# A group norm and attention kernel: the setup and the first image in another order

## What is computed

```python
h = group_norm(x)                       # 32 groups of 8 channels, per image
q, k, v = h @ Wq + bq, h @ Wk + bk, h @ Wv + bv
scores = einsum('bnc,bmc->bnm', q, k) * 256 ** -0.5
attn = softmax(scores, axis=-1)
out = x + einsum('bnm,bmc->bnc', attn, v) @ Wo + bo
```

## Time and profile before

| what | value |
|---|---|
| median of 3 runs | 1845.19 us (1845.04 to 1846.48) |
| profiled execution | 1844.48 us, of which the span 1842.8 us |
| PE busy | 1815.6 us, 99% of the span |
| DVE busy | 1663.2 us, 90% |
| ACT busy | 984.1 us, 53% |
| mean granted PE clock | 0.994 |

### The profile page before, as it was taken

How to read it: one execution, slowest core, us unless ns; L and a number is a source line. 1 busy time by engine, 2 the same in 40 slices (tenths; PEclk the granted TensorE clock), 3 DMA queues, 4 the chain that set the end, 5 groups by cost and what they waited for, 6 DMA issues and landing times.

```text
span 1842.8 us, 32692 instructions
## 1 busy us (share of the span) xinstructions
PE 1815.6 (99%) x11562; PEld 1654.1 (90%) x11562; DVE 1663.2 (90%) x2921; ACT 984.1 (53%) x1347; POOL 92.1 (5%) x107
## 2 busy tenths in 40 slices
PE   8899999999999999999999999999999999999997
PEld 7799998999998998989999989989989999899896
DVE  5999999999999999999999999999999999999985
ACT  3645545646546556456455465465564554654652
POOL 0000000000000000000000000000000000000000
PEclk9999999999999999999999999999999999999998
DMA  3111222212222212222122222022221122220211
GB/s 114 58 51 29 68 57 68 68 26 54 68 57 68 62 18 68 57 68 68 36 44 68 57 68 67 12 68 62 63 68 43 37 68 57 68 68 17 62 24 24
DMA packets 29296, 101.92 MB, mean 55 GB/s; under 512 B 3681, under 2 KB 4706, under 8 KB 29282
## 3 DMA queue, kind: packets, MB, share of 16 engines
q0 software_dynamic: 9216, 33.56, 11.7%
q1 hardware_dynamic: 20066, 68.17, 11.2%
HBM read 68.16 MB, written 67.11 MB: 73 GB/s over the span
## 4 chain that ended last, share of the span: by engine, by line
PE 98%; DVE 1%; ACT 0%; DMA 0%; issue 0%; SPq 0%; POOLq 0%
PE ps_s L619 48%; PE ps_o L693 13%; PE ps_o L695 13%; PE ps_o L694 13%; PE ps_o L619 10%; DMA s_buf<-in_L_conv_bq_dram 0%; ACT p_hi L312 0%; ACT s_buf L318 0%; DVE s_buf L485 0%; DVE p_lo L493 0%; PE ps_o L631 0%; DVE s_buf L510 0%; DVE query_max L472 0%; SPq L217 0%; POOLq L66 0%
## 5 line engine op out<-in xcount | busy, mean ns | idle before, releaser
L693 PE MATMUL ps_o<-v_hi,p_hi 128*128 128x258 f32 x2048 | 580.6, 283 | 2.8 <-DVE p_lo L493 2.8
L695 PE MATMUL ps_o<-v_hi,p_lo 128*128 128x258 f32 x2048 | 581.1, 284 | 0.0
L694 PE MATMUL ps_o<-v_lo,p_hi 128*128 128x256 f32 x2048 | 578.4, 282 | 0.0
L312 ACT ACTIVATE p_hi<-s_buf 128x1024 fp32r<-128x1024 f32 x256 | 272.0, 1063 | 527.5 <-DVE s_buf L485 527.5
L619 PE MATMUL ps_s<-g_hi,h_hi 128*128 128x512 f32 x1024 | 399.7, 390 | 7.8 <-ACT s_buf L304 7.7
L619 PE MATMUL ps_s<-g_hi,h_lo 128*128 128x512 f32 x1024 | 400.4, 391 | 0.0
L619 PE MATMUL ps_s<-g_lo,h_hi 128*128 128x512 f32 x1024 | 399.8, 390 | 0.0
L693 PEld LDWEIGHTS ps_o<-v_hi,p_hi 128*128 128x128 f32 x2048 | 389.2, 190 | 5.7 <-issue 2.2
L694 PEld LDWEIGHTS ps_o<-v_lo,p_hi 128*128 128x128 f32 x2048 | 388.9, 190 | 3.0
L695 PEld LDWEIGHTS ps_o<-v_hi,p_lo 128*128 128x128 f32 x2048 | 388.7, 190 | 0.0
L304 ACT ACTIVATE s_buf<-ps_s 128x512 f32<-128x512 f32 x512 | 292.9, 606 | 170.2 <-PE ps_s L619 166.3
(11 more groups left out here) (84 smaller groups left out, 2199.5 us busy)
## 6 DMA issues: line engine op xcount, KB each, us to landing
x_t<-in_x_turned_dram SPq DMA_DIRECT2D x64, 512.0 KB, 3.9
out_dram<-in_x_dram SPq DMA_DIRECT2D x64, 512.0 KB, 7.3
out_dram<-o_buf POOLq DMA_DIRECT2D x64, 512.0 KB, 5.6
s_buf<-in_L_conv_Wq_dram SPq DMA_DIRECT2D x1, 256.0 KB, 3.0
s_buf<-in_L_conv_Wk_dram SPq DMA_DIRECT2D x1, 256.0 KB, 3.0
s_buf<-in_L_conv_Wv_dram SPq DMA_DIRECT2D x1, 256.0 KB
s_buf<-in_L_conv_Wo_dram SPq DMA_DIRECT2D x1, 256.0 KB
s_buf<-in_L_conv_bq_dram SPq DMA_DIRECT2D x1, 1.0 KB, 3.1
```

Of the source, the lines that this page charges most:

```text
L312: nc.scalar.activation(p_hi[c][:, rows, :], s_buf[c][:, rows, :], ACT.Exp, scale=SCALE).then_inc(p_hi_done, 1)
L693: nc.tensor.matmul(ps[:, 0:VC], p_hi[c][:, m, cols], v_hi[:, m, :], start=m == 0, stop=False)
L694: nc.tensor.matmul(ps[:, 0:C], p_hi[c][:, m, cols], v_lo[:, m, :], start=False, stop=False)
L695: last = nc.tensor.matmul(ps[:, 0:VC], p_lo[c][:, m, cols], v_hi[:, m, :], start=False, stop=m == T - 1)
```

## The change

SP issues `x_t` of image 0 ahead of the weights, and the three short bias vectors behind them with semaphores of their own. PE multiplies two constant tiles twelve times into an unused bank, then transposes all three weights and does both folds ahead of `project_g`. ACT, no longer DVE, copies the transposed weights out. In image 0, `normalise`, `h_parts` and `h_rest` work by halves of 512 tokens, half 0 first. DVE now does the whole group norm of image 1 between `g_rest` and `part_maxima` of image 0, and the `v_lo` parts after the first `difference`. ACT puts the copies of the first four score tiles of half 1 between the exponentials of half 0. The loop over images 1 to 30 and the last image are untouched.

```diff
+            load_turned(0)
             load_weight(0, wq, wqk_in)
             load_weight(1, wk, wqk_in)
-            with nc.allow_non_contiguous_dma(reason="a short vector, once"):
-                sp.dma_start(bq_col, bq.rearrange("(k p) -> p k", p=P)).then_inc(wqk_in, 16)
-            load_turned(0)
             load_weight(2, wv, wvo_in)
             load_weight(3, wo, wvo_in)
...
+                sp.dma_start(bq_col, bq.rearrange("(k p) -> p k", p=P)).then_inc(bq_in, 16)
+                sp.dma_start(bv_col, bv.rearrange("(k p) -> p k", p=P)).then_inc(bias_in, 16)
+            sp.dma_start(bo_row, bo.rearrange("(a n) -> a n", a=1)).then_inc(bias_in, 16)
...
+            turned_out(0)
+            turned_out(1)
+            turned_out(2)
+            first_h_part(0, 0, first_h, first_h_hi)
+            first_h_part(1, 0, first_h, first_h_hi)
+            fold_first(a_hi, ps_a, 1)
+            first_h_part(0, 1, h_done, h_hi_done)
+            first_h_part(1, 1, h_done, h_hi_done)
+            fold_first(vo_hi, ps_vo, 3)
...
+            def first_softmax():
+
+                for i in range(4):
+                    v_part(0, i)
+                exponentials_hi(0, 0, 0)
+                scores_out(0, 1, 0)
+                exponentials(0, 0, 0)
+                scores_out(0, 1, 1)
+                exponentials_hi(0, 0, 1)
+                scores_out(0, 1, 2)
+                exponentials(0, 0, 1)
+                scores_out(0, 1, 3)
+                for i in (2, 3):
+                    exponentials_hi(0, 0, i)
+                    exponentials(0, 0, i)
+                for m in range(4, T):
+                    scores_out(0, 1, m)
...
+            first_normalise(0, 0, first_h)
+            first_normalise(1, 0, first_h)
+            first_normalise(0, 1, h_done)
+            first_normalise(1, 1, h_done)
+            first_h_rest(0, 0, first_h_hi, first_h_lo)
+            first_h_rest(1, 0, first_h_hi, first_h_lo)
+            fold_rest(0, a_hi, a_lo, ps_a)
+            dve.wait_ge(bias_in, 16 * 2)
...
+                channel_stats(1)
+                dve.wait_ge(bn_done, 8)
+                channel_sums(1)
+                group_means(1)
+                group_spread(1)
+                maxima(0, 0, 0)
+                group_variance(1)
+                maxima(0, 0, 1)
+                turn_back(1)
+                maxima(0, 0, 2)
+                normalise(1)
+                maxima(0, 0, 3)
+                maxima(0, 0, 4)
...
-            pe.wait_ge(wqk_in, 16 * 3)
             pe.wait_ge(const_step, 7)
+            for _ in range(12):
+                nc.tensor.matmul(ps_idle[:, 0:P], ident[:], ones[:], start=True, stop=True)
+            pe.wait_ge(wqk_in, 16 * 2)
             turn_weight(0)
             turn_weight(1)
-
+            pe.wait_ge(wvo_in, 16 * 2)
+            turn_weight(2)
             pe.wait_ge(w_turned, 2)
             fold(ps_a, wq_t, wk_t)
```

More of the change, by code:

```diff
@@ L287, in h_parts, with first_h_part @@
                     nc.scalar.activation(h_hi[:, k, :], x_t[:, k, :], ACT.Copy).then_inc(h_hi_done, 1)
+            def first_h_part(k, c, ready, done):
+                act.wait_ge(ready, k + 1)
+                cols = slice(c * Q, (c + 1) * Q)
+                nc.scalar.activation(h_hi[:, k, cols], x_t[:, k, cols], ACT.Copy).then_inc(done, 1)
             def g_part(b, i):
@@ L354, in body @@
                 if first:
[L355 to L361, removed]
+                    first_softmax()
+                else:
+                    softmax_beside(b, 0, lambda i: v_part(b, i))
+                    scores_out(b, 1, 0)
+                    last_exponentials(b, 0)
+                    for m in range(1, T):
+                        scores_out(b, 1, m)
                 if not last:
@@ L424, in normalise, with first_normalise, first_h_rest @@
                                             ALU.subtract, ALU.mult).then_inc(h_done, 1)
+            def first_normalise(k, c, done):
+                cols = slice(c * Q, (c + 1) * Q)
+                nc.vector.tensor_scalar(x_t[:, k, cols], x_t[:, k, cols], norm[:, 0, k:k + 1], norm[:, 1, k:k + 1],
+                                        ALU.subtract, ALU.mult).then_inc(done, 1)
+            def first_h_rest(k, c, ready, done):
+                cols = slice(c * Q, (c + 1) * Q)
+                dve.wait_ge(ready, k + 1)
+                nc.vector.tensor_tensor(h_lo[:, k, cols], x_t[:, k, cols], h_hi[:, k, cols].bitcast(F32),
+                                        ALU.subtract).then_inc(done, 1)
             def h_rest(b, k):
@@ L544, in _, with second_stats, first_softmax @@
                 g_rest(0, i)
+            def second_stats():
+                channel_stats(1)
[11 more added lines that the diff above has]
+                maxima(0, 0, 4)
+            def first_softmax():
+                part_maxima(0, 0)
+                query_maxima(0, 0)
+                row_maxima(0, 0)
+                difference(0, 0, 0)
+                for i in range(4):
+                    v_rest(0, i)
+                difference(0, 0, 1)
+                p_rest(0, 0, 0)
+                difference(0, 0, 2)
+                p_rest(0, 0, 1)
+                difference(0, 0, 3)
+                p_rest(0, 0, 2)
+                p_rest(0, 0, 3)
             def softmax_beside(b, c, finish_tile, h_next, project, next_stats, next_sums):
@@ L575, in next_stats @@
                     dve.wait_ge(bn_done, b * 4 + 8)
-                for step in range(5):
-                    maxima(b, 0, step)
                 if first:
-                    next_stats()
-                    for i in range(4):
-                        v_rest(b, i)
-                    channel_sums(b + 1)
-                    softmax_beside(b, 0, nothing, nothing, nothing, nothing, nothing)
-                elif last:
+                    second_stats()
+                    first_softmax()
+                else:
+                    for step in range(5):
+                        maxima(b, 0, step)
+                if last:
                     softmax_beside(b, 0, lambda j: finish(b - 1, 1, j), nothing, lambda i: v_rest(b, i),
                                    nothing, nothing)
-                else:
+                elif not first:
                     softmax_beside(b, 0, lambda j: finish(b - 1, 1, j), nothing, lambda i: v_rest(b, i),
                                    next_stats, lambda: channel_sums(b + 1))
-                if not last:
+                if not first and not last:
                     group_means(b + 1)
```

65 lines of the change are left out of this document (33 added, 32 removed).

## The result

Six runs of the kernel before have a median of 1844.50 us (1843.68 to 1846.48). Of six runs of the changed kernel one took 9163.25 us and is left out of the comparison; the other five lie between 1835.92 and 1837.21, and the median is 1836.78. The two medians differ by 7.7 us. The ratio on record is 0.9951 with a 95% interval of 0.9940 to 0.9961, which is a gain of 7.2 to 11.1 us: the change makes the kernel faster, and the last microsecond or two of the size are not certain.

The account below looks back on a forecast made before the run. PE was taken to bound the kernel, with time to win only in the setup and about the first softmax: 3.2 + 6.2 = 9.4 us off 1844.48 gives 1835.1 profiled, 1835.8 as median; own range 1834 to 1837.5, 8 in 10 1833.3 to 1840.8.

Parts of the forecast that it names:

- The two parts of the sum: 3.2 us from an earlier first `project_g` and 6.2 us about the first softmax, 9.4 us together.
- G: Start of the first `project_g`, end of the setup: 17.5 instead of 20.72, 3.2 us earlier.
- `x_t` lands, 6.3: Setup: with `x_t` issued first, DVE's last three statistics start at 6.3 instead of 9.22.
- DVE to G, 17.4: Setup: DVE's chain from x's landing to `bv_wide` at 15.8, then PE's `out_bias` of 1.6, ends at 17.4.
- Weights at 7.7: Setup: Wq and Wk, queued behind x, land about 7.7, within 1 us either way.
- The clock in the folds: Setup: PE's clock taken as up, folds ending near 14.4; the term is 3.2 us if up, nothing if not.
- folds at half clock: Rival, setup: G stays near 20.7, only 6.2 us remain, 1839.0 us; chance 0.36.
- DVE's stretch, 33.5: About the first softmax: DVE's path to the end of image 1's `h_lo` shrinks from 39.72 to 33.5, gaining 6.2 us.
- The new waits, 1.8 and 1.8: PE about the first softmax: waits of 1.8 us for `v_lo` and 1.8 for `h_lo` replace 7.65.
- The clock in a new hole: Rival: the clock falls in a new PE wait, costing 2.0 to 3.4 us, 1837.8 to 1842.4; chance 0.11.
- Everything carries over: Untouched loop: whatever image 1 starts earlier comes off the end whole; the rival, nothing carries over, had 0.01.
- The last image spared: Rival, last image: the clock does not fall at PE's 2.0 us wait, 3.4 us less, 1832.4; chance 0.05.

Follow-up runs that it names:

- e11: The changed kernel itself, run again beside e12 on one chip; 1835.17 us, 0.9948 of the kernel before.
- e2: New setup of the changed kernel, with ACT's and DVE's order from the first softmax on as in the kernel before; 1840.92 us, 0.9982.
- e3: Setup of the kernel before, with the changed kernel's order from the first softmax on; 1840.33 us, 0.9975.
- e6: Changed kernel with Wq and Wk issued ahead of `x_t` of image 0 again; 1841.63 us, 0.9978 of the kernel before.
- e10: As e6, with PE's first fold also put ahead of the wait for Wv and Wo; 1842.04 us, 0.9987.
- e4: Changed kernel with nine constant products filling PE's wait at the second `project_g`; 1835.25 us, 0.9948 of the kernel before.
- e5: Changed kernel with `h_lo` of image 1 moved ahead of the second softmax of image 0; 1835.57 us, 0.9945 of the kernel before.
- e7: Changed kernel with 22 constant products instead of 12; 1834.96 us, 0.9942 of the kernel before.
- e12: The order of e9 again, run beside e11 on one chip; 1833.45 us, 0.9937 of the kernel before.
- e1: Changed kernel without its twelve constant products; 1837.59 us, 0.9961 of the kernel before.
- e8: Changed kernel with DVE's two `bv_wide` products moved into its wait for POOL's power; 1835.35 us, 0.9946 of the kernel before.
- e9: e8 with 16 constant products, `h_lo` of image 1 early as in e5, and image 1's `g` parts moved up; 1833.57 us, 0.9941.

## Why the prediction was right, point by point

The forecast was 1835.8 us, 9.4 below before; measured are 7.7 and, in e11, 10.0 below. The forecast was the likeliest case of several, at 0.44, and the run was not it in pure form: half clock came in the setup and in a new hole, and both cost less than they had been priced at. The two parts of the sum hold, and e2 and e3 show each by itself. The profiled execution came 2.1 us over the forecast 1835.1, and the table shows where: 0.1 at G, 0.4 on the way to the second `project_g`, 1.1 by the fall there, 0.4 behind the third.

- **`x_t` lands, 6.3.** Mis-sized: 5.69. The two gains together are 3.5 us (from 9.22), no run parts them, and e6 and e10 show the price of the old order.
- **DVE to G, 17.4.** The chain had the right links and was 0.7 long, by the landing above: where DVE was last, G was 16.65 to 16.85. In the first profile G was 17.62 for another reason, PE being late, so that the agreement with 17.5 is in part luck: the DVE term was 0.7 too small a gain, and PE took that 0.7 away.
- **Weights at 7.7.** Between 7.4 and 9.3 from one execution to the next. Each microsecond there costs up to one at G, once PE is the later of the two.
- **The clock in the folds,** the forecast's chief bet, with "folds at half clock" at 0.36. Neither case as stated: it was up for e2, e4, e5, e7 to e12, and at half from 9.01 to 12.42 in the first profile, where the folds took 5.31 instead of 4.5 us. The prediction priced the rival at nothing left of the 3.2 us. The folds' first 1.5 us at half clock cost 0.8. That the gain wants the clock is shown by e1: at half clock, by their spacing of 0.43 us, up to 14.87 us the folds took 6.04 us, and G was 19.40, only 1.3 us under before; 0.8 of what is missing goes with the weights' late landing. At half clock throughout, as in e6, they take 8.38.
- **DVE's stretch, 33.5.** Measured 33.94; the waits for exponentials are 1.1 us, not 0.3, and the rest of the stretch is 0.4 shorter than worked out. The statistics of image 1 were covered as said: the second step of the maxima came at G + 14.74 (forecast 14.76).
- **The new waits, 1.8 and 1.8.** Measured 1.55 for `v_lo` and 2.09 for `h_lo`. DVE was late next, as the prediction had it, and G to the second `project_g` was 48.8 (48.4). PE's own way there had been put at 46.5; e5, without the second wait, took 46.63.
- **The clock in a new hole.** The step that failed. The prediction had the clock at 1.00 behind both holes: "The two holes of 1.8 us are shorter than the 2.0 us that went with a fall" gave this rival 0.11; the second hole was 2.09 us, no shorter, and the fall came in five of eight executions with it (not in e7, e8 and e10). Its price was wrong too, 2.0 to 3.4 us by the length of the low stretches of before; it lasted 3.41 us and cost 1.1. So the rival occurred and its cost stayed inside the forecast's own range, 1834 to 1837.5: that the median fell there is in part luck. The upper end of the rival's range, 1842.4, does not follow from its own terms, since 1.6 and 3.4 us on 1835.8 give 1840.8.
- **Everything carries over.** Shown by the column "3rd to end": 1711 us of loop returned what they were given, within 0.4. **The last image spared:** e2 and e4 had no fall there, worth 1.3 to 1.7 us and not 3.4.

What stays open is why the same wait of 2.09 us goes with a fall in one execution and not in another. In e7, e8 and e10 it did not, in e11 it did, and the programs around it are alike from the first `project_g` on. The changed kernel, the only one of these programs profiled twice, fell both times; so the record does not rule out that the program decides, by what its setup does. Nor does any run take out the halves of 512 tokens or ACT's copies of the transposed weights alone: their share of the 3.1 us is argued from DVE's chain and not measured.

## What to carry to other kernels

Where PE bounds a loop with no waits, look for the stalls at its edges and read how far the next engine is behind: here 7.65 us of wait were worth 5.8 up to the next `project_g`, because DVE was next, 2 us behind. In a setup, issue first the load with the longest chain behind it, even if the engine that bounds the kernel then waits longer for its own. Moving a late operation ahead (e5) handed the wait to what it passed; with that moved too (e9), the waits shrank from 2.1 to 0.9 us and the kernel gained 0.8 us.

## What was not expected of the hardware

- Landing times of the same DMAs, in the same order, spread over almost 2 us between executions (the first transposes of weights at 7.45, 8.55 and, without tiles ahead, 9.32), enough to change which engine sets G.
- POOL's power of image 1, four elements a partition, took 2.03 us before and 1.01 in the changed kernel. Before, it started at 61.95 beside DVE's maximum of 1024 elements, which ran from 61.88 to 63.11; now it runs from 31.18, while DVE waits. e2, with the old order, has 1.92 again (from 57.87, beside DVE's maximum from 57.70 to 58.93), and e3, with the new one, 1.01. So 0.9 to 1.0 us more goes with such a maximum beside it; what holds POOL up, no run shows.
- Half clock behind short waits: 1.90 us in the setup, 2.09 at the second `project_g`, and in e4 a fall behind a wait of 1.1 us among small products, where e11 had none behind 1.26 us at the same place. With 1.55 us between long matmuls (the wait for `v_lo`) there was none in any of twelve executions.
